# One subtraction between two stages, copies ahead of exponentials in four batches, and the own-token transposes first

## The chip, the cores and the metric

The kernel runs on one core of a Trainium2 chip. The metric is the device time of one execution in microseconds (us). The profile is one execution recorded by the hardware profiler: its span runs from the first to the last instruction.

## The reference

Four layers, each added to its input. `x` has 64 batches of 64 tokens of 512 numbers. The stage that the change touches is the third layer (attention over a cache of key and value blocks, 8 query heads on 4 key/value heads of 64, a window of 256 keys) with its output projection `Wo`, and the fourth (a small matrix per batch).

```
x = x + _L0_cond_ref(x, itok_B_0_15, L0_cond_W, L0_cond_b)
x = x + _L1_cond_ref(x, L1_cond_W, L1_cond_A, L1_cond_Bm, L1_cond_scalings, itok_B_0_6)
x = x + _L2_cond_ref(x, L2_cond_Wq, ..., itok_Bx257_0_4111, itok_B_37_3939)
x = x + _L3_cond_ref(x, itok_B_0_7, L3_cond_weights, fside_8xS_0)
...
scores = jnp.einsum('bghtd,bgsd->bghts', qg, k_all) * SCALE
scores = jnp.where(allowed[:, None, None, :, :], scores, -jnp.inf)
p = jax.nn.softmax(scores, axis=-1)
o = jnp.einsum('bghts,bgsd->bghtd', p, v_all).reshape(Bx, H, Tx, HD)
o = o.transpose(0, 2, 1, 3).reshape(Bx, Tx, H * HD)
return jnp.einsum('bto,do->btd', o, Wo)
```

## The kernel before

The kernel has two stages, each a software pipeline written out by hand. Every engine has its own program, and only semaphores tie them together. An engine works through its program strictly in the order in which it is written, so an instruction that waits holds all that stand behind it.

Stage one (`phase_one`, 32 pairs of batches, until about 514 us) computes layers 0 and 1 and the queries, keys and values of layer 2. It writes new keys and values to `new_rows` in DRAM.

Stage two (`phase_two`) runs once for each of the 64 batches, with a few steps more for what trails behind. Step `b` works on several batches at once. The names below are those of the code.

- **GpSimd (POOL)** gathers the keys and values of later batches into `ring` (called `kv` there): `gather_new` issues three indirect DMAs for each batch (L535, then L546 twice), `gather_old` one (L499). They are paced by semaphores of the batches in work.
- **TensorE (PE)**, step `b`: `scores(b)` (L753, twelve records in the profile, into three PSUM banks); `transpose_keys(b+1, .., 0)` (L730, L731); on even steps from 4 on the second half of `project` (L802); `transpose_probs` of batch `b-1` (L771: eight 128x128 transposes of window probabilities in two groups of four; L777: two of the batch's own 64 tokens); `transpose_keys(b+1, .., 1)`; on odd steps from 3 on the first half of `project`; on even steps the matmul of layer 3 (L838); `values` of batch `b-1` (L790, L795), which waits for all three copies of transposed probabilities.
- **ScalarE (ACT)**: copies the transposed keys from PSUM into `kt` (`copy_keys`, L920, once for each of two halves; `scores(b+1)` waits for both); takes four exponentials (`exps`, L930); copies the second group of transposed probabilities and the own ones (`copy_second` L937, `copy_own` L942, into `pt` and `pt2`); copies the attention output (`ot_hi`, L964). How many of the four exponentials stand ahead of the probability copies is `early`: one on odd steps, all four on even ones. The second copy of keys stands behind all of them.
- **VectorE (DVE)**: adds the mask and takes the row minimum for four heads' groups (`masked`, L1236); copies the first group of transposed probabilities (`copy_first`, L1218), behind all four `masked` on even steps and between them on odd ones; on even steps from 4 on adds into `x3` (L1261); scales the four groups of probabilities (L1272), each adding one to `prob_ready`; makes the next mask (L1205, L1206); computes the remainder of the attention output (`ot_lo`, L1224).

`Wo` is used as two parts: `wo_hi`, which ScalarE makes at L913 between the stages, and the remainder `wo_lo` (L1279), four subtractions of 128x512 each. `wo_lo` is first read by `project` of step 3.

The semaphore `pt_done` counts three for each batch, one at the end of each group of transposes. Whoever copies a group waits for its number, and `gather_new` and the exponentials of a later batch wait for the third.

Of the kernel before, what the change touches and what calls it, by code (L numbers as in the profile page):

```python
# [4 lines left out]
F32 = mybir.dt.float32  # L5
# [50 lines left out]
def build(nc, a):  # L56

    ctx = ExitStack()
    with ctx:
# [187 lines left out]
        def wait(eng, semaphore, value):  # L247

            if not isinstance(value, int) or value > 0:
                eng.wait_ge(semaphore, value)  # L250
# [309 lines left out]
        def _(pe):  # L560
# [177 lines left out]
            def phase_two(b, j, s):  # L738
# [25 lines left out]
                def transpose_probs():  # L764

                    for p, copied in ((0, pt0_ready), (1, pt1_ready)):
                        pe.wait_ge(prob_ready, G * b - G + 2 * p + 2)
                        wait(pe, copied, b - 1)
                        for q in range(2):
                            for c in range(2):  # L770
                                last = nc.tensor.transpose(ps_pt[p][:, (q * 2 + c) * P:(q * 2 + c + 1) * P],  # L771
                                                           prob[:, r % 2, (5 * p + 3 * q + c) * P:(5 * p + 3 * q + c + 1) * P], ident[:, :])
                        last.then_inc(pt_done, 1)
                    wait(pe, pt2_ready, b - 1)
                    wait(pe, ot_ready, b - 1)
                    for p in range(GP):
                        last = nc.tensor.transpose(ps_pt2[:, p * P:(p + 1) * P], prob[:, r % 2, (5 * p + 2) * P:(5 * p + 3) * P], ident[:, :])  # L777
                    last.then_inc(pt_done, 1)

# [67 lines left out]
        def _(act):  # L847
# [77 lines left out]
            def phase_two(b, j, s):  # L925
# [7 lines left out]
                def copy_second():  # L933

                    act.wait_ge(pt_done, 3 * b - 1)
                    wait(act, pv_done, b - 1)
                    nc.scalar.activation(pt[:, 1, :, :, :].rearrange("p q c t -> p (q c t)"), ps_pt[1][:, :], ACT.Copy).then_inc(pt1_ready, 1)  # L937

                def copy_own():

                    act.wait_ge(pt_done, 3 * b)
                    nc.scalar.activation(pt2[:, :, :].rearrange("p q t -> p (q t)"), ps_pt2[:, 0:GP * P], ACT.Copy).then_inc(pt2_ready, 1)  # L942

                if on(b, -1, NB):
                    copy_keys(b + 1, s + 1, 0)
                early = 1 if s % 2 == 1 else G
                if on(b, 0, NB):
                    for g in range(early):
                        exps(g)
                if on(b, 1, NB):  # L950
                    copy_second()
                    copy_own()
                if on(b, 0, NB):
                    for g in range(early, G):
                        exps(g)
                if on(b, -1, NB):
                    copy_keys(b + 1, s + 1, 1)
# [13 lines left out]
        def _(dve):  # L971
# [230 lines left out]
            def make_mask(b, s):  # L1202
# [4 lines left out]
                                ALU.is_lt, ALU.mult).then_inc(mask_ready, 1)  # L1207

            dve.wait_ge(ld_late, 16)
            dve.wait_ge(ld_mask, 4 * 16)  # L1210
            make_mask(0, 0)

            def phase_two(b, j, s):
                def copy_first():

                    dve.wait_ge(pt_done, 3 * b - 2)
                    wait(dve, pv_done, b - 1)
                    V.tensor_copy(pt[:, 0, :, :, :].rearrange("p q c t -> p (q c t)"), ps_pt[0][:, :]).then_inc(pt0_ready, 1)  # L1218
# [55 lines left out]
                if on(b, -1, NB):  # L1274
                    make_mask(b + 1, s + 1)
                if isinstance(b, int) and b < 2:
                    dve.wait_ge(wo_hi_ready, 1)
                    for c in range(2 * b, 2 * b + 2):
                        V.tensor_tensor(wo_lo[:, c, :], wo_stage[:, c, :], wo_hi[:, c, :].bitcast(F32), ALU.subtract).then_inc(wo_lo_ready, 1)  # L1279
                if on(b, 1, NB):  # L1280
# [78 lines left out]
```

## Time and profile before

| what | value |
|---|---|
| median of 3 runs | 975.33 us (974.92 to 979.87) |
| time of the profiled execution | 973.05 us |
| its span | 970.5 us |
| TensorE busy | 935.1 us (96%) |
| VectorE busy | 604.6 us (62%) |
| ScalarE busy | 383.8 us (40%) |
| GpSimd busy | 513.4 us (53%) |

The span is 2.55 us under that execution's own time, and the median of the three runs is 2.28 us above it. TensorE is busy nearly all the time; the stretches in which it is not are where the order of the other engines can matter.

### The profile page before, as it was taken

The numbers are of one execution on the slowest core, as the hardware profiler recorded it, in microseconds if no ns is written. First come the engines' busy times: TensorE is split into PE (matmuls) and PEld (weight loads), VectorE is DVE, ScalarE is ACT, GpSimd is POOL, SyncE is SP. The second block draws the span as 40 slices with busy tenths as digits, with TensorE's granted clock in tenths as the row PEclk, the third lists the DMA queues.
The fourth block names the chain that finished last, engine by engine and source line by source line (L and its number), as shares of the span: only waits on it lengthen the run. The fifth ranks groups of instructions, "written<-read, shape, count | busy, mean of one in ns | idle before, by whom it ended". The sixth has DMA issues, their size and how long they took to land.

```text
span 970.5 us, 22302 instructions
## 1 busy us (share of the span) xinstructions
PE 935.1 (96%) x6253; PEld 690.1 (71%) x6253; DVE 604.6 (62%) x1788; ACT 383.8 (40%) x1061; POOL 513.4 (53%) x469
## 2 busy tenths in 40 slices
PE   6899999999999999999996899999999999999998
PEld 4566766667666676676765677778778788787785
DVE  6434344657566554446643677777777787777875
ACT  2121221212212122121213556566565665666653
POOL 1255464454644558745366566555665555555530
PEclk9999999999999999999998999999999999999999
DMA  9789888686786776867645565665666666666641
GB/s 305 267 278 306 276 304 277 211 271 224 253 280 220 258 247 229 279 229 253 231 141 164 150 195 176 194 207 175 197 184 192 209 204 198 181 195 210 206 136 45
DMA packets 105162, 212.48 MB, mean 219 GB/s; under 512 B 29563, under 2 KB 52056, under 8 KB 96930
## 3 DMA queue, kind: packets, MB, share of 16 engines
q1 hardware_dynamic: 71042, 145.54, 44.4%
q0 software_dynamic: 25088, 57.74, 20.0%
q10 hardware_dynamic: 8992, 8.73, 2.8%
q8 instruction: 17, 0.28, 0.1%
q14 instruction: 23, 0.19, 0.1%
HBM read 204.39 MB, written 33.86 MB: 245 GB/s over the span
## 4 chain that ended last, share of the span: by engine, by line
PE 92%; DMA 2%; issue 2%; DVE 1%; ACT 1%; POOL 1%; SPq 1%; DVEq 0%; POOLq 0%; ACTq 0%
PE banks L587 11%; PE banks L802 9%; PE banks L705 9%; PE banks L753 9%; PE banks L790 7%; PE banks L626 6%; PE banks L634 6%; PE banks L636 6%; PE banks L771 6%; PE banks L730 4%; PE banks L795 4%; PE banks L695 3%; PE banks L838 3%; PE banks L710 3%; PE banks L597 2%
## 5 line engine op out<-in xcount | busy, mean ns | idle before, releaser
L546 POOL DMA_INDIRECT ring<-new_rows,idx x128 | 130.0, 1016 | 84.1 <-DVE big L1272 54.8
L458 POOL TENSOR_TENSOR rms<-ss,neg_half 128x12 f32<-128x12 f32 x31 | 70.8, 2285 | 175.5 <-DVE ss L1181 175.5
L930 ACT ACTIVATE big<-big,neg_max 128x320 f32<-128x320 f32 x256 | 141.3, 554 | 2.7 <-DVE neg_max L1236 2.5
L1236 DVE CUSTOM_DVE_ANT_0 big<-banks,mask 128x320 f32<-128x320 f32 x256 | 114.7, 486 | 36.0 <-PE banks L753 33.2
L587 PE MATMUL banks<-ring 128*64 128x512 f32 x512 | 117.1, 599 | 2.7 <-DMA ring<-in_w 2.7
L871 ACT ACTIVATE x2t_hi<-banks 128x512 fp32r<-128x512 f32 x32 | 19.1, 597 | 235.2 <-PE banks L597 235.2
L920 ACT ACTIVATE kt<-banks 128x384 f32<-128x384 f32 x128 | 62.1, 485 | 100.7 <-PE banks L731 100.7
L753 PE MATMUL banks<-kt,q_in 64*128 64x128 f32 (+2 forms) x768 | 89.0, 365 | 3.1 <-ACT kt L920 3.1
L587 PEld LDWEIGHTS banks<-ring 128*64 128x64 f32 x512 | 34.1, 136 | 81.0 <-issue 79.9
L535 POOL DMA_INDIRECT ring<-new_rows,idx x64 | 61.5, 961 | 55.1 <-PE banks L777 51.2
L1272 DVE TENSOR_SCALAR big<-big,recip 128x320 f32<-128x320 f32 x256 | 86.0, 398 | 2.3
L790 PEld LDWEIGHTS banks<-pt,ring 128*64 128x64 f32 x1024 | 55.9, 137 | 43.9 <-issue 27.8
L753 PEld LDWEIGHTS banks<-kt,q_in 64*128 64x128 f32 x768 | 74.7, 190 | 16.5 <-issue 14.5
L499 POOL DMA_INDIRECT ring<-in_kvrows,idx x64 | 61.2, 956 | 41.8 <-PE banks L753 24.5
L1134 DVE TENSOR_TENSOR x<-banks,x_in 128x512 f32<-128x512 f32 x32 | 22.1, 691 | 95.1 <-PE banks L587 90.9
L790 PE MATMUL banks<-pt,ring 128*64 128x128 f32 x1024 | 70.6, 279 | 7.7 <-ACT pt L942 3.3
L903 ACT ACTIVATE sq<-banks 128x512 f32<-128x512 f32 x31 | 18.6, 600 | 130.8 <-PE banks L636 130.8
L448 POOL TENSOR_TENSOR x_in<-x_in,bias_in 128x512 f32<-128x512 f32 x32 | 41.6, 1301 | 51.5 <-DMA ring<-in_rope 45.2
L771 PE MATMUL banks<-ident,big 128*128 128x128 f32 x512 | 67.5, 275 | 0.2 <-DVE big L1272 0.2
L634 PE MATMUL banks<-wqkv_hi,x2t_lo 128*128 128x512 f32 x248 | 66.4, 390 | 0.0
L636 PE MATMUL banks<-wqkv_lo,x2t_hi 128*128 128x512 f32 x248 | 66.3, 389 | 0.0
L626 PE MATMUL banks<-wqkv_hi,x2t_hi 128*128 128x512 f32 x248 | 65.4, 405 | 0.7 <-ACT x2t_hi L871 0.7
(169 smaller groups left out, 1982.8 us busy)
## 6 DMA issues: line engine op xcount, KB each, us to landing
ring<-in_w SPq DMA_DIRECT2D x62, 1024.0 KB, 6.0
ring<-in_xt SPq DMA_DIRECT2D x32, 256.0 KB, 2.7
x_in<-in_x SPq DMA_DIRECT2D x32, 256.0 KB, 5.6
bias_in<-in_b SPq DMA_DIRECT2D x64, 128.0 KB, 5.4
x_dram<-x SPq DMA_DIRECT2D x32, 256.0 KB, 5.0
q_dram<-q_t ACTq DMA_DIRECT2D x32, 256.0 KB, 2.3
new_rows<-kv_out SPq DMA_DIRECT2D x32, 256.0 KB, 4.8
q_in<-q_dram SPq DMA_DIRECT2D x64, 128.0 KB
```

The source lines that it names most:

```text
L546: pool.indirect_dma_start(out=kv[:, s, c, :], out_offset=None, in_=new_rows, in_offset=bass.IndirectOffsetOnAxis(ap=idx[:, b, 1 + c:2 + c] ...
L587: last = nc.tensor.matmul(ps_l0[T * h:T * h + T, :], xt[:, s, c, T * h:T * h + T], w0[:, 2 * s + h, c * D:(c + 1) * D], start=(c == 0), st ...
L626: nc.tensor.matmul(ps_out[:, :], x2t_hi[:, c, :], wqkv_hi[:, c, n0:n0 + D], start=(c == 0), stop=False)
L634: nc.tensor.matmul(ps_out[:, :], x2t_lo[:, c, :], wqkv_hi[:, c, n0:n0 + D], start=False, stop=False)
L636: last = nc.tensor.matmul(ps_out[:, :], x2t_hi[:, c, :], wqkv_lo[:, c, n0:n0 + D], start=False, stop=(c == DC - 1))
L705: nc.tensor.matmul(ps_l1[:, :], x_part[:, c, :], w_part[:, c, :], start=(c == 0 and x_part is x1t_hi and w_part is w1_hi), stop=False)
L753: return nc.tensor.matmul(banks[:, S0[g] + n0:S0[g] + n1], q_in[r0:r0 + HD, s % 4, g // 2, :], kt[r0:r0 + HD, s % 2, g // 2, k0 + n0:k0 + ...
L771: last = nc.tensor.transpose(ps_pt[p][:, (q * 2 + c) * P:(q * 2 + c + 1) * P], prob[:, r % 2, (5 * p + 3 * q + c) * P:(5 * p + 3 * q + c + ...
L790: nc.tensor.matmul(ps_o[HD * q:HD * q + HD, p * P:(p + 1) * P], kv[:, r, c, v0:v0 + HD], pt[:, p, q, c, :], start=(c == 0 and p == 0), sto ...
L802: last = nc.tensor.matmul(out[:, n0:n1], o_part[:, pair_s, c, :], w_part[:, c, n0:n1], start=(c == 0 and n == 0), stop=(c == DC - 1 and n ...
L930: nc.scalar.activation(prob[:, s % 2, g * NK:(g + 1) * NK], sm[:, s % 2, g, :], ACT.Exp, bias=neg_max[:, s % 2, g:g + 1], scale=-1.0, accu ...
L1236: V.tensor_tensor_reduce(sm[:, s % 2, g, :], ps_s[g], mask[:, s % 2, k0:k0 + NK], 1.0, 3.0e38, ALU.add, ALU.min, accum_out=neg_max[:, s % ...
```

## The change

Four edits in stage two:

1. The four subtractions for `wo_lo` leave the steps `b` = 0 and 1 (two in each, behind the mask) and stand between the stages, behind stage one and ahead of the first mask.
2. In steps 0 to 3 (`ramp`) ScalarE does one exponential, then the probability copies, then the second copy of keys, then the other three exponentials.
3. `transpose_probs` does the two own-token transposes first, then the two groups of four. All ten now stand behind the waits that the own ones had (`ot_ready`, `pt2_ready`) and behind one wait for all four scaled groups; before, each group of four waited for two of them more.
4. In every step ScalarE makes `copy_own` ahead of `copy_second`.

```diff
                 def transpose_probs():
+                    pe.wait_ge(prob_ready, G * b)
+                    wait(pe, pt2_ready, b - 1)
+                    wait(pe, ot_ready, b - 1)
+                    for p in range(GP):
+                        last = nc.tensor.transpose(ps_pt2[:, p * P:(p + 1) * P], prob[:, r % 2, (5 * p + 2) * P:(5 * p + 3) * P], ident[:, :])
+                    last.then_inc(pt_done, 1)
                     for p, copied in ((0, pt0_ready), (1, pt1_ready)):
-                        pe.wait_ge(prob_ready, G * b - G + 2 * p + 2)
                         wait(pe, copied, b - 1)
...
-                    wait(pe, pt2_ready, b - 1)
-                    wait(pe, ot_ready, b - 1)
-                    for p in range(GP):
-                        last = nc.tensor.transpose(ps_pt2[:, p * P:(p + 1) * P], prob[:, r % 2, (5 * p + 2) * P:(5 * p + 3) * P], ident[:, :])
-                    last.then_inc(pt_done, 1)
...
-                early = 1 if s % 2 == 1 else G
+                ramp = isinstance(b, int) and b < 4
+                early = 1 if s % 2 == 1 or ramp else G
                 if on(b, 0, NB):
                     for g in range(early):
                         exps(g)
                 if on(b, 1, NB):
+                    copy_own()
                     copy_second()
-                    copy_own()
+                if ramp:
+                    copy_keys(b + 1, s + 1, 1)
                 if on(b, 0, NB):
                     for g in range(early, G):
                         exps(g)
-                if on(b, -1, NB):
+                if not ramp and on(b, -1, NB):
                     copy_keys(b + 1, s + 1, 1)
...
+            dve.wait_ge(wo_hi_ready, 1)
+            for c in range(DC):
+                V.tensor_tensor(wo_lo[:, c, :], wo_stage[:, c, :], wo_hi[:, c, :].bitcast(F32), ALU.subtract).then_inc(wo_lo_ready, 1)
             dve.wait_ge(ld_late, 16)
             dve.wait_ge(ld_mask, 4 * 16)
             make_mask(0, 0)
...
-                if isinstance(b, int) and b < 2:
-                    dve.wait_ge(wo_hi_ready, 1)
-                    for c in range(2 * b, 2 * b + 2):
-                        V.tensor_tensor(wo_lo[:, c, :], wo_stage[:, c, :], wo_hi[:, c, :].bitcast(F32), ALU.subtract).then_inc(wo_lo_ready, 1)
```

The waits of the three copies on `pt_done` are renumbered to the new order.

ScalarE, steps 0 and 1 (and the beginning of step 2), before and then with the change; `kt` is a copy of keys, `big` an exponential, `pt` a copy of probabilities:

```order
L930 ACTIVATE big,row_sum<-big,neg_max 128x320 x4
L920 ACTIVATE kt<-banks 128x384 x2
L930 ACTIVATE big,row_sum<-big,neg_max 128x320
L937 ACTIVATE pt<-banks 128x512
L942 ACTIVATE pt<-banks 128x256
L930 ACTIVATE big,row_sum<-big,neg_max 128x320 x3
L920 ACTIVATE kt<-banks 128x384
L964 ACTIVATE ot_hi<-banks 128x4x64
```

```order
L930 ACTIVATE big,row_sum<-big,neg_max 128x320
L920 ACTIVATE kt<-banks 128x384
L930 ACTIVATE big,row_sum<-big,neg_max 128x320 x3
L920 ACTIVATE kt<-banks 128x384
L930 ACTIVATE big,row_sum<-big,neg_max 128x320
L942 ACTIVATE pt<-banks 128x256
L937 ACTIVATE pt<-banks 128x512
L920 ACTIVATE kt<-banks 128x384
L930 ACTIVATE big,row_sum<-big,neg_max 128x320 x3
L967 ACTIVATE ot_hi<-banks 128x4x64
```

In each step one copy of keys moved from behind the last exponential to behind the first, and the small copy (`pt`, 256 wide) moved ahead of the large one.

VectorE, from the last instructions of stage one to the first `masked` of stage two, before and then with the change:

```order
L1117 TENSOR_TENSOR q_rot<-ring,rms 128x512
L1119 COPY scol<-scol 128x1
L1205 COPY mask<-beyond 128x1
L1206 TENSOR_SCALAR mask<-iota,first_key 128x255
L1236 ISA big,neg_max<-banks,mask 128x320
```

```order
L1120 TENSOR_TENSOR q_rot<-ring,rms 128x512
L1122 COPY scol<-scol 128x1
L1214 TENSOR_TENSOR wo_lo<-stage,wo_hi 128x512 x4
L1208 COPY mask<-beyond 128x1
L1209 TENSOR_SCALAR mask<-iota,first_key 128x255
```

The four subtractions now stand directly behind the last instruction of stage one.

TensorE in step 1, from the transposes of keys ahead of `transpose_probs` to `values`, before and then with the change:

```order
L730 MATMUL banks<-ident,ring 128x128 x2
L731 MATMUL banks<-ident,ring 128x2x64
L771 MATMUL banks<-ident,big 128x128 x8
L777 MATMUL banks<-ident,big 128x128 x2
L730 MATMUL banks<-ident,ring 128x128 x2
L731 MATMUL banks<-ident,ring 128x2x64
L790 MATMUL banks<-pt,ring 64x128 x8
```

```order
L730 MATMUL banks<-ident,ring 128x128 x2
L731 MATMUL banks<-ident,ring 128x2x64
L770 MATMUL banks<-ident,big 128x128 x2
L776 MATMUL banks<-ident,big 128x128 x8
L730 MATMUL banks<-ident,ring 128x128 x2
L731 MATMUL banks<-ident,ring 128x2x64
L790 MATMUL banks<-pt,ring 64x128 x8
```

The two own transposes (128 wide, x2) moved ahead of the eight of the window, and nothing else moved. GpSimd's and SyncE's programs are the same in both kernels.

## Rows read from the trace of the kernel before

**Rows 1.** The page: the span.

```profile
span 970.5 us, 22302 instructions
```

**Rows 2.** Busy time by stretch: engines in their order, PEclk, DMA share, GB/s.

```profile
520.00:540.00 20.00, 14.42 (x97) 11.84 (x98) 9.96 (x35) 8.66 (x26) 11.00 (x12) 0.74 0.52 152
540.00:560.00 20.00, 16.75 (x140) 13.31 (x140) 14.15 (x52) 11.90 (x38) 11.48 (x12) 0.91 0.52 155
560.00:580.00 20.00, 19.89 (x185) 16.05 (x180) 14.39 (x51) 12.48 (x39) 12.39 (x13) 1.00 0.58 172
```

**Rows 3.** Timeline of TensorE: start, duration, what, idle before and its releaser.

```profile
523.84 2.50 PE L753 MATMUL banks<-kt,q_in 64*128 64x128 f32 x12 [0.67 <-ACT kt L920]
...
530.39 1.86 PE L753 MATMUL banks<-kt,q_in 64*128 64x128 f32 x12 [2.09 <-ACT kt L920]
...
544.35 1.63 PE L790 MATMUL banks<-pt,ring 128*64 128x128 f32 x16 [2.84 <-ACT pt L942]
...
546.96 1.93 PE L753 MATMUL banks<-kt,q_in 64*128 64x128 f32 x12
...
552.12 1.09 PE L790 MATMUL banks<-pt,ring 128*64 128x128 f32 x16
...
553.73 1.35 PE L753 MATMUL banks<-kt,q_in 64*128 64x128 f32 x12
```

**Rows 4.** The page's costliest groups: busy, mean ns of one, idle before.

```profile
L930 ACT ACTIVATE big<-big,neg_max 128x320 f32<-128x320 f32 x256 | 141.3, 554 | 2.7 <-DVE neg_max L1236 2.5
L920 ACT ACTIVATE kt<-banks 128x384 f32<-128x384 f32 x128 | 62.1, 485 | 100.7 <-PE banks L731 100.7
```

**Rows 5.** Timeline of VectorE in steps 0 to 2.

```profile
531.86 1.29 DVE L1279 TENSOR_TENSOR wo_lo<-stage,wo_hi 128x512 fp32r<-128x512 f32 x2
...
537.49 1.27 DVE L1272 TENSOR_SCALAR big<-big,recip 128x320 f32<-128x320 f32 x4
...
539.00 1.29 DVE L1279 TENSOR_TENSOR wo_lo<-stage,wo_hi 128x512 fp32r<-128x512 f32 x2
...
540.54 0.48 DVE L1236 CUSTOM_DVE_ANT_0 big<-banks,mask 128x320 f32<-128x320 f32 x1
```

**Rows 6.** Timelines between the stages: ScalarE, VectorE, GpSimd.

```profile
511.16 1.92 ACT L913 ACTIVATE wo_hi<-stage 128x2048 fp32r<-128x2048 f32 x1 [0.55 <-ACT q_t L857]
...
516.97 0.15 DVE L1205 COPY mask<-beyond 128x1 f32<-128x1 f32 x1 [3.15 <-DMA mask<-in_own]
...
514.29 1.03 POOL L546 DMA_INDIRECT ring<-new_rows,idx  x1 [0.30 <-issue]
```

**Rows 7.** The chain that ended last, in order of time: start, duration, what.

```profile
515.62 5.08 DMA ring<-new_rows,idx
```

**Rows 8.** Timelines of GpSimd and VectorE at three indirect DMAs.

```profile
387.08 1.30 POOL L441 DMA_INDIRECT table_i<-writer,win_both  x1 [0.16 <-issue]
...
531.83 1.00 POOL L546 DMA_INDIRECT ring<-new_rows,idx  x1 [0.92 <-DVE big L1272]
...
539.27 1.90 POOL L546 DMA_INDIRECT ring<-new_rows,idx  x1 [1.80 <-PE banks L753]
...
386.72 0.75 DVE L1162 TENSOR_TENSOR x1t_lo<-x1t,x1t_hi 128x512 fp32r<-128x512 f32 x1 [0.77 <-ACT x1t L879]
```

**Rows 9.** VectorE and TensorE in a step of the steady part.

```profile
561.58 0.42 DVE L1224 TENSOR_TENSOR ot_lo<-banks,ot_hi 128x256 fp32r<-128x256 f32 x1 [1.24 <-ACT ot_hi L964]
...
562.64 1.04 PE L771 MATMUL banks<-ident,big 128*128 128x128 f32 x8
```

**Rows 10.** TensorE and VectorE behind the last scores.

```profile
956.51 1.25 PE L771 MATMUL banks<-ident,big 128*128 128x128 f32 x8 [0.24 <-DVE big L1272]
957.60 0.38 PE L777 MATMUL banks<-ident,big 128*128 128x128 f32 x2
...
960.84 1.09 PE L790 MATMUL banks<-pt,ring 128*64 128x128 f32 x16 [1.45 <-DVE pt L1218]
...
956.96 0.42 DVE L1224 TENSOR_TENSOR ot_lo<-banks,ot_hi 128x256 fp32r<-128x256 f32 x1
```

More of the change, by code:

```diff
@@ L933, in copy_second @@
                 def copy_second():
-                    act.wait_ge(pt_done, 3 * b - 1)
+                    act.wait_ge(pt_done, 3 * b)
                     wait(act, pv_done, b - 1)
@@ L939, in copy_own @@
                 def copy_own():
-                    act.wait_ge(pt_done, 3 * b)
+                    act.wait_ge(pt_done, 3 * b - 2)
                     nc.scalar.activation(pt2[:, :, :].rearrange("p q t -> p (q t)"), ps_pt2[:, 0:GP * P], ACT.Copy).then_inc(pt2_ready, 1)
@@ L1214, in copy_first @@
                 def copy_first():
-                    dve.wait_ge(pt_done, 3 * b - 2)
+                    dve.wait_ge(pt_done, 3 * b - 1)
                     wait(dve, pv_done, b - 1)
```

## The prediction, before the changed kernel was run

> **What bounds the kernel now.** I read the view by stretches first. From 560 us on TensorE is busy 19.89 us of 20 at the full granted clock [rows 2]: there the time is TensorE's work, which the change neither adds to nor takes from. Around the border of the stages it is not: 14.42 us of 520 to 540 and 16.75 us of 540 to 560, at a mean clock of 0.74 and 0.91 of 2.4 GHz [rows 2], so some stretches ran at 1.2 GHz. TensorE's timeline says what it waits for there. Between the batches' first scores (523.84) and those of batch 4 (553.73) it waits 2.09 us for the second copy of keys and 2.84 us for the copies of probabilities [rows 3]. The reader is to see the cost at the slow clock too: sixteen `values` matmuls take 1.63 us at 544.35 against 1.09 at 552.12, and a set of scores 1.93 at 546.96 against 1.35 at 553.73 [rows 3]. From 553.73 on the steps follow each other with no wait worth the name. So what the change can win lies between 523.84 and 553.73, 29.9 us for four batches. What it can lose lies ahead of it, in the wait of each steady step, and at the end.
>
> **The ramp, edits 1, 2 and 3 together.** I follow the order by hand, on the clock of the profile, with TensorE at 2.4 GHz. Durations: an exponential each 0.55, a copy of keys 0.49 [rows 4]; four `masked` some 1.7 (0.48 each, overlapping a little) [rows 5]; scaling and next mask together 1.5 (539.00 minus 537.49) [rows 5]; `ot_lo` 0.42 [rows 9]; ten transposes 1.1 (1.04 for eight with overlap) [rows 9]; scores 1.35, `values` with its own part 1.6 (553.73 minus 552.12) [rows 3]; transposes of a half of keys some 0.35 to 0.45, estimated from their three matmuls.
> Step 0: scores end at 526.3 [rows 3]. One exponential ends at 528.15, the second half of keys is transposed by 528.35 and copied by 528.9. `scores(1)` start at 529.0 instead of 530.39, 1.4 us earlier. The price is that the other three exponentials end at 530.5 instead of 529.8, and batch 0's probabilities are scaled by 532.2.
> Step 1: edit 3 makes even the first transpose wait for all four scaled groups, so TensorE, done with scores and keys at 530.8, idles until 532.25. It ends the ten at 533.35. `masked(1)` starts at 532.5, with no `wo_lo` ahead of it (1.29 us before [rows 5]). Exponential to 533.6, own copy, second copy from 533.7 to 534.3. `values(0)` runs from 534.4 to 536.0, scores 2 to 537.35. ScalarE, behind the copy of keys (534.7), ends the exponentials at 536.3. Scaling and mask last until 538.1, `ot_lo(0)` until 538.5.
> Step 2: four `masked` from 538.5 to 540.1, against a start of 540.54 behind the second pair of subtractions [rows 5]. The transposes wait for `ot_lo` and run from 538.55 to 539.65. Before, all four exponentials stood ahead of the copies and `values(1)` started at 544.35 [rows 3]. Now ScalarE's copies are done at 540.2, and what comes last is VectorE's `copy_first` behind the four `masked`, at 540.8 (0.7 us long, estimated from 0.42 for half the width [rows 9]). `values(1)` starts at 540.9, 3.5 us earlier, `scores(3)` at 542.5 instead of 546.96, 4.5 us earlier.
> Step 3: exponentials end at 542.2, scaling and mask at 544.0, `ot_lo(1)` at 544.4; ten transposes to 545.55, keys, half a projection (1.4), `values(2)` to 548.9. `scores(4)` start there instead of 553.73: **4.8 us earlier**. Behind it TensorE is the bound, as before, and an offset is kept to the end.
> That is with the clock at 2.4 GHz throughout. In this account TensorE still waits 1.45, 0.8, 1.2 and 0.9 us, and before, the clock fell behind gaps of 2.09 and 2.84 us. If `values(2)` and what follows run at 1.2 GHz as they partly did for batch 1 before, the two differences above, 0.54 for sixteen matmuls and 0.58 for a set of scores, with a like amount in its small neighbours, give back 1.1 to 1.8 us. Bounds of the ramp: a gain of 3.0 to 4.8 us. I take 4.3, since the new gaps are all shorter than the two behind which the clock fell.
>
> **Edit 1 at its new place.** `wo_hi` is complete at 513.08, VectorE is free at 513.8 (its idle time of 3.15 us ends at 516.97) [rows 6], so four subtractions (2.5 us, from two of 1.29) end at 516.3 and hold nobody on VectorE. But GpSimd issues the indirect DMAs for batch 0 at that very time: one at 514.29 [rows 6], the last at 515.62. TensorE's first transposes wait for that last one, which lands at 520.70 [rows 7], which is on the chain that ended last. There are two longer indirect DMAs that began while a VectorE subtraction of two SBUF tensors was running. The one at 539.27 took 1.90 us and the subtractions ended at 540.29, 1.02 after it began; the one at 387.08 took 1.30 and the subtraction (386.72 plus 0.75) ended 0.39 after it began [rows 5, 8]. The one at 514.29 took 1.03 with VectorE idle. The excess, 0.87 and 0.27, is nearly what was left of the subtraction. With the subtractions in progress until 516.3, the DMA at 514.29 would finish near 517.3 instead of 515.3, and the one behind it as much later: 2.0 us at most. Below, nothing: where GpSimd's instruction began first, it is not held (531.83, 1.00 us, with a subtraction from 531.86 on [rows 5, 8]). Landing may slip less than the issue, as the 5.08 us contain traffic of other queues. I take **1.6 us later**, near the upper end, because both rows with this order of starts show it.
> The Trainium skill, page "GPSIMD Engine Reference", section "1. Specifications", says the SBUF interfaces are shared with VectorE, with contention for instructions with two SBUF inputs. By that rule the full hold of 2.0 us would be counted, where a reading that VectorE's idle time is free gives 0. The two rows agree with it in kind.
>
> **Edit 3 in the steady part.** The own transposes waited for `ot_lo` behind the eight; now the eight wait as well. In the tight steps (the ones with no projection ahead) `ot_lo` ends at 562.00 and the transposes start at 562.64 [rows 9]: 0.64 us to spare, and scaled probabilities are older still. Cost 0, hidden by scores and keys. If that cover were gone, each 0.1 us would count some thirty times. Edit 4 in the steady part only swaps two neighbours on ScalarE whose last end is what `values` waits for: 0. `gather_new` waits for the third count of `pt_done`, still the end of all ten transposes: 0.
>
> **Edit 3 at the end.** For the last batch no scores hide the wait. The eight started at 956.51 with two of four groups scaled, the own two at 957.60 [rows 10]. Now nothing starts before `ot_lo` is done (956.96 plus 0.42, 957.38), so ten transposes run from 957.42 to 958.5 instead of ending at 957.8. Behind them stand the projection, the sum on VectorE, its copy and `values` at 960.84, one chain to the end [rows 10]. Loss **0.7 us**, between 0.5 and 0.9.
>
> **The sum.** Minus 4.3, plus 1.6, plus 0.7 is minus 2.0 us. Against the profiled execution (973.05, its span of 970.5 [rows 1] and 2.55 around it) that is 971.05; the median of the runs shown lies 2.28 above it, so 973.3.
>
> **Rivals.**
> *The forecast* (0.50): entry held by 1 to 2 us, ramp 3.5 to 4.8: net minus 0.8 to minus 3.1, so 972.2 to 974.5.
> *No hold of the gathers* (0.20): for it speaks the DMA at 531.83, not lengthened; against it the order of starts, since here the subtractions begin at 513.8 and the DMA at 514.29. Net minus 2.8 to minus 4.1: 971.2 to 972.5.
> *The clock falls again, or rises later* (0.13): TensorE's start lies later, so the slow stretch within 520 to 540 [rows 2] can reach further, and the new gaps add up. Ramp 2 to 3, entry 2, tail 0.7: net 0 to plus 0.7, with a second slow stretch up to plus 2: 975.3 to 977.3.
> *The edits are swallowed* (0.07): keys and values are gathered only a little ahead, and GpSimd's last gather for batch 3 waits for scaled probabilities of batch 0, which come 0.65 us later in my account. It was issued at 531.83 in 1.00 us [rows 8], and the one of batch 0 landed 4.1 us after its issue ended (520.70 minus 516.6 [rows 7]). So it lands near 537.6, where TensorE wants it at 537.35. If landings grow longer than that, step 2 and its followers hang on them, the ramp's gain is 1 to 2 us, and entry and tail eat it: 975 to 976.5.
> *The other side, a steady wait* (0.07): transposes of the tight steps wait for `ot_lo` in the new order. It decides once the 0.64 us are used up; at 0.2 us over, thirty such steps cost 6 us, less 2.0: 979.3.
> *A larger gain* (0.03): no hold and a ramp above 4.8, TensorE's weight loads closing up: below 970.5.
>
> **How the numbers follow.** 973.3 is the first case. The range of 8 in 10 joins the first two and most of the third: 970.9 to 976.6. This kernel's measurement tells about 0.5% (4.9 us) from no change. Faster by more needs nearly the whole ramp with no cost at either end: 0.05. Slower by more needs the steady wait or a clock much worse: 0.06. Within 0.5%: 0.89.
>
> **What would show it.** In the changed profile: first transposes of keys near 522.4 and an indirect DMA of some 3 us near 514.3 (wrong if 520.8 and 1.0); `scores(1)` 5.2 us behind `scores(0)` instead of 6.55; `scores(4)` 25 us behind `scores(0)` instead of 29.9; no wait of TensorE for `ot_lo` between 560 and 950; the last `values` 0.7 us later against the last scores. The prediction is wrong if the clock is low in more of these 25 us than before, or if a steady step is longer than before by a trace of a wait, since thirty of them outweigh all the rest.

## The result: 965.4 us, 0.9% faster

| | before | changed |
|---|---|---|
| median | 975.12 us (973.02 to 979.87, 4 runs) | 965.41 us (962.48 to 966.05, 4 runs) |
| ratio | | 0.9911, interval 0.9882 to 0.9941 |
| profiled execution, its span | 973.05, 970.5 us | 962.48, 960.7 us |

The gain is 9.7 us where I had put 2.0. The page of the changed kernel, its span and its engines:

```profile
span 960.7 us, 22134 instructions
...
PE 931.3 (97%) x6253; PEld 687.7 (72%) x6253; DVE 604.0 (63%) x1788; ACT 383.8 (40%) x1061; POOL 512.8 (53%) x469
```

Busy time by stretch of the changed kernel, columns as in [rows 2]:

```profile
500.00:520.00 20.00, 16.34 (x92) 13.47 (x90) 11.45 (x29) 4.85 (x7) 13.81 (x13) 0.91 0.54 179
520.00:540.00 20.00, 13.23 (x124) 10.53 (x126) 10.44 (x41) 11.77 (x36) 13.68 (x14) 1.00 0.61 184
540.00:560.00 20.00, 19.23 (x174) 15.54 (x172) 14.98 (x53) 12.88 (x42) 12.69 (x13) 1.00 0.57 161
560.00:580.00 20.00, 20.00 (x176) 15.83 (x174) 16.75 (x58) 13.00 (x41) 10.90 (x13) 1.00 0.69 207
```

Two things differ from [rows 2]. From 520 us on the clock is full, where it was 0.74 and 0.91: from 520 to 540, 13.23 busy us of TensorE hold 124 matmuls where 14.42 held 97. And 560 to 580 shows 20.00 busy of 20 where [rows 2] has 19.89: the steady part has lost its small gaps. TensorE's timeline, start, duration, what, idle before and its releaser:

```profile
520.80 0.41 PE L730 MATMUL banks<-ident,ring 128*128 128x128 f32 x2 [0.95 <-DMA ring<-new_rows,idx]
...
523.11 1.36 PE L753 MATMUL banks<-kt,q_in 64*128 64x128 f32 x12 [0.67 <-ACT kt L920]
...
526.75 1.35 PE L753 MATMUL banks<-kt,q_in 64*128 64x128 f32 x12 [0.67 <-ACT kt L920]
...
530.00 0.44 PE L770 MATMUL banks<-ident,big 128*128 128x128 f32 x2 [1.02 <-DVE big L1278]
...
532.38 1.10 PE L790 MATMUL banks<-pt,ring 128*64 128x128 f32 x16 [0.74 <-ACT pt L937]
...
536.63 0.41 PE L770 MATMUL banks<-ident,big 128*128 128x128 f32 x2 [0.80 <-DVE ot_lo L1230]
...
538.78 1.09 PE L790 MATMUL banks<-pt,ring 128*64 128x128 f32 x16 [0.54 <-DVE pt L1224]
...
547.54 1.35 PE L753 MATMUL banks<-kt,q_in 64*128 64x128 f32 x12
```

The waits of 2.09 and 2.84 us in [rows 3] are gone, `scores(4)` start 24.4 us behind `scores(0)` instead of 29.9, and the waits that edit 3 adds are there, shorter than in my account: 1.02 and 0.80 us for 1.45 and 1.2. Where the 9.9 us between the ends of the last instructions (968.31 and 958.43) lie:

| stretch | before | changed | difference |
|---|---|---|---|
| start to `scores(0)` | 523.84 | 523.11 | -0.7 |
| `scores(0)` to `scores(4)` | 29.89 | 24.43 | -5.5 |
| `scores(4)` to `scores(60)` | 375.97 | 371.67 | -4.3 |
| `scores(60)` to the last end | 38.61 | 39.22 | +0.6 |

The third row was to be 0. It is 0.15 us in each of 28 pairs of batches, all of it in the even step. There TensorE waits with `values` for ScalarE's two copies: in all 28 even steps of the first profile for which both rows are there, `values` start 0.62 us behind the small copy's start. First before, TensorE and ScalarE (the view ends at 573.5, so three of the sixteen matmuls are not in its second row):

```profile
571.66 1.02 PE L838 MATMUL banks<-bias_in,bd 128*128 128x512 f32 x2
572.79 0.95 PE L790 MATMUL banks<-pt,ring 128*64 128x128 f32 x13
...
571.69 0.57 ACT L937 ACTIVATE pt<-banks 128x512 f32<-128x512 f32 x1
572.17 0.37 ACT L942 ACTIVATE pt<-banks 128x256 f32<-128x256 f32 x1
```

Then the changed kernel:

```profile
552.04 1.02 PE L838 MATMUL banks<-bias_in,bd 128*128 128x512 f32 x2
553.02 1.09 PE L790 MATMUL banks<-pt,ring 128*64 128x128 f32 x16
...
552.07 0.37 ACT L942 ACTIVATE pt<-banks 128x256 f32<-128x256 f32 x1
552.33 0.58 ACT L937 ACTIVATE pt<-banks 128x512 f32<-128x512 f32 x1
```

The pair of copies takes 0.85 us by its rows in the one order (571.69 to 572.54) and 0.84 in the other (552.07 to 552.91): by the last end the swap is worth nothing, as I had counted. But `values` start 0.25 us after the last end before and 0.11 us after it now; from L838 to L790 it is 1.13 and 0.98. With the large copy last, `values` stand directly behind L838 and no gap is left. That some 0.68 and 0.62 us from a copy's start are what TensorE needs at least shows where it clearly waits for the copy: 532.38 above is 0.68 behind the large copy's start (531.70), 544.35 in [rows 3] is 0.61 behind the small one's (543.74).

### The profile page after: what moved, and what is told of

It reads as the page before. It is cut to its first block, busy times and chain, and to the rows that moved or that the text cites. A ratio compares the mean times of both kernels' runs of the same rounds, so it can differ in the third digit from the quotient of the medians.

```text
span 960.7 us, 22134 instructions
## 1 busy us (share of the span) xinstructions
PE 931.3 (97%) x6253; PEld 687.7 (72%) x6253; DVE 604.0 (63%) x1788; ACT 383.8 (40%) x1061; POOL 512.8 (53%) x469
## 4 chain that ended last, share of the span: by engine, by line
PE 91%; SPq 3%; DMA 2%; issue 1%; DVE 1%; ACT 1%; POOL 0%; DVEq 0%; POOLq 0%; ACTq 0%
PE banks L587 11%; PE banks L802 9%; PE banks L705 9%; PE banks L753 8%; PE banks L790 7%; PE banks L626 6%; PE banks L634 6%; PE banks L636 6%; PE banks L776 6%; PE banks L795 4%; PE banks L730 4%; PE banks L838 3%; PE banks L695 3%; PE banks L710 3%; PE banks L597 2%; PE banks L770 1%
## 5 line engine op out<-in xcount | busy, mean ns | idle before, releaser
L546 POOL DMA_INDIRECT ring<-new_rows,idx x128 | 129.4, 1011 | 82.2 <-DVE big L1278 55.5
L753 PE MATMUL banks<-kt,q_in 64*128 64x128 f32 (+2 forms) x768 | 86.8, 358 | 1.3 <-ACT kt L920 1.3
L753 PEld LDWEIGHTS banks<-kt,q_in 64*128 64x128 f32 x768 | 72.8, 187 | 14.3 <-issue 12.4
L790 PEld LDWEIGHTS banks<-pt,ring 128*64 128x64 f32 x1024 | 55.2, 137 | 37.7 <-DVE pt L1224 23.3
L790 PE MATMUL banks<-pt,ring 128*64 128x128 f32 x1024 | 70.0, 278 | 2.7 <-DVE pt L1224 2.0
```

Of the source, the lines that this page charges most:

```text
L546: pool.indirect_dma_start(out=kv[:, s, c, :], out_offset=None, in_=new_rows, in_offset=bass.IndirectOffsetOnAxis(ap=idx[:, b, 1 + c:2 + c] ...
L753: return nc.tensor.matmul(banks[:, S0[g] + n0:S0[g] + n1], q_in[r0:r0 + HD, s % 4, g // 2, :], kt[r0:r0 + HD, s % 2, g // 2, k0 + n0:k0 + ...
L790: nc.tensor.matmul(ps_o[HD * q:HD * q + HD, p * P:(p + 1) * P], kv[:, r, c, v0:v0 + HD], pt[:, p, q, c, :], start=(c == 0 and p == 0), sto ...
```

## The experiments

The tables read three stretches out of each profile: from the first L753 to the reciprocal on VectorE of batch 6 (**ramp**), from there to that of batch 60, by 27 (**pair**: two batches of the steady part), and from there to the last end (**tail**). In the two kernels so far: before 47.98, 13.424, 34.05; changed 42.36, 13.270, 34.66.

### One edit at a time

The kernel before with edit 4 alone:

```diff
-                    copy_second()
                     copy_own()
+                    copy_second()
```

> The kernel before with edit 4 alone: in every step ScalarE makes the 256-wide own copy ahead of the 512-wide second copy. Theory A (what edit 4 saves in the steady part is the time from the last copy's start to TensorE's values matmul: before, the small copy started 0.48 us behind the large one and values started 0.62 us after that, 1.10 in all; with the small one first the large one starts 0.26 later and values 0.69 after that, 0.95): the distance of scores over two batches falls from 13.43 to 13.27 us, and the whole is 4 to 5 us faster, ratio near 0.995. Theory B (it is the order of the transposes on TensorE, edit 3, that closed the wait): 13.43 us stays, ratio 1.000.

With edit 3 alone (its diff as shown above, the copies' waits renumbered):

> The kernel before with edit 3 alone: own transposes first and all ten behind four scaled groups and ot_lo; ScalarE still makes the large copy first. Theory A: 13.43 us for two batches stays, and only the end is later, by 0.6 to 0.7 us; ratio 1.000 to 1.001. Theory B: two batches take 13.27 us, ratio near 0.996.

With edit 2 alone:

```diff
-                early = 1 if s % 2 == 1 else G
+                ramp = isinstance(b, int) and b < 4
+                early = 1 if s % 2 == 1 or ramp else G
...
+                if ramp:
+                    copy_keys(b + 1, s + 1, 1)
...
-                if on(b, -1, NB):
+                if not ramp and on(b, -1, NB):
```

> The kernel before with edit 2 alone: in steps 0 to 3 one exponential, copies of probabilities, copy of keys, three exponentials. Theory A (most of the gain between the scores of batch 0 and batch 4, 5.5 us with the whole change, is edit 2): 4 to 5 us of it here, two batches still 13.43, ratio near 0.995. Rival (without edit 1 the second pair of wo_lo subtractions still stands ahead of batch 2's masks and takes most of it): 2 us or less, ratio above 0.997.

With edit 1 alone (the four subtractions between the stages, none in steps 0 and 1):

> The kernel before with edit 1 alone: the four subtractions between the stages. Theory A: they are off the path in their new place, one indirect DMA is lengthened by 0.3 to 0.5 us and the landing TensorE waits for doesn't slip; on the old place they cost 0.6 us in step 0 and 1.2 in step 1, so scores 0 to scores 4 are 1 to 2 us shorter, ratio 0.998 to 0.999. Rival, my forecast's term: the start of scores 0 is 1.6 us later, ratio 1.000.

On this and the next two occasions the kernel before itself took 1005 to 1008 us and not 975. They ran on the chips numbered 6, 11 and 6; the last two occasions below, where it took 973.6 and 977.5, ran on the chips 0 and 8. For the first pair no chip is on record.

| kernel | median, us | ratio to before | ramp | pair | tail |
|---|---|---|---|---|---|
| before | 1007.7 | | | | |
| edit 4 | 1004.93 | 0.9977 (0.9957 to 0.9997) | 49.67 | 14.517 | 34.31 |
| edit 3 | 1011.23 | 1.0042 (1.0027 to 1.0057) | 50.02 | 14.806 | 35.85 |
| edit 2 | 1005.27 | 0.9975 (0.9958 to 0.9993) | 48.60 | 14.620 | 34.94 |
| edit 1 | 1007.09 | 0.9993 (0.9976 to 1.001) | 48.16 | 14.532 | 34.96 |

A pair of batches takes 1.1 us more than in either of the first two profiles, whatever the edit. So the runs could not say what they were made for; edit 3 alone costs 3.5 us here, the others are within 0.3%. Edit 2 alone was to bring 4 to 5 us in the ramp and edit 1 alone 1 to 2. Against the 49.29 of the kernel before in the same condition (measured below) they bring 0.7 and 1.1, and edits 1, 2 and 4 together (46.65, on chip 11) 2.6. TensorE's clock in the ramp differs between these profiles (the first scores take 1.36 us with edit 2 alone, 2.50 with edit 1 alone and 2.47 in the kernel before), so these shares are not separated.

### What holds every kernel at 1005 us

The changed kernel again, edit 4 again, a variant, and edits 1, 2 and 4. The variant is the kernel before with three exponentials ahead of the copies on even steps, so that both copies are early enough in either order:

```diff
-                early = 1 if s % 2 == 1 else G
+                early = 1 if s % 2 == 1 else G - 1
```

> The changed kernel once more, beside the others, as the measure for them. If two batches take 13.3 to 13.4 us in the steady part as in the first two profiles: ratio 0.989 to 0.994. If TensorE pauses inside the scores as in the four profiles taken since (two batches 14.3 us), the wait that edit 4 closes lies under that pause, so theory A gives only the part before the scores of batch 4, ratio 0.995.

> The kernel before with edit 4 alone, again, since the first look at it was taken where two batches took 14.3 us. Theory A: where the steady part runs without the pause, two batches take 13.27 us instead of 13.43, ratio 0.995. Theory B: 13.43, ratio 1.000.

> The kernel before with three instead of all four exponentials ahead of the probability copies on even steps, and the copies in the old order. It closes the same wait in another way. Theory A (values on even steps wait for ScalarE's last copy, 0.15 us): the copies come 0.55 us earlier, two batches take 13.27 us, ratio 0.994 to 0.995. Theory B (TensorE's own order): 13.43, ratio 1.000 or worse, since the fourth exponential and the scaled probabilities come 0.75 us later.

> The changed kernel without edit 3: the eight window transposes first, as before, the rest as changed. Theory A (edit 3 brings nothing in the steady part and costs 0.6 us at the end): steady part as with the whole change, 0.5 to 1 us faster than it through the end and the ramp, where transposes no longer wait for ot_lo. Theory B: two batches fall back to 13.43 us, 4 us slower than the whole change.

| kernel | median, us | ratio to before (1005.0) | ramp | pair | tail |
|---|---|---|---|---|---|
| changed | 1006.12 | 1.002 (0.9996 to 1.0044) | 48.53 | 14.623 | 35.16 |
| edit 4 | 1004.81 | 0.9991 (0.9973 to 1.001) | 49.24 | 14.505 | 34.82 |
| three early | 1003.58 | 0.999 (0.9969 to 1.0012) | 50.05 | 14.494 | 33.17 |
| edits 1, 2, 4 | 1002.9 | 0.9973 (0.9951 to 0.9994) | 46.65 | 14.527 | 34.78 |

Here the change brings nothing, and what edit 4 won is not there either: something else ends last. For the same reason the variant with three exponentials could not tell its two theories apart. To see what, the kernel before with a profile of this condition, the changed kernel a third time, and the kernel before with one gather less per batch (the keys and values at odd places of the new rows are left out, so that part of the attention is computed on old data):

> The kernel before itself, traced in the condition of the later runs (about 1005 us instead of 975), to have a reference for them. If that condition is one of the machine and not of the edits, it has the same late signals: once in two batches ScalarE's ot_hi starts 1.3 us or more later behind the last values matmul than the 0.7 us (from its start) of the first profile, and two batches take 14.5 us; ratio 1.000.

> The changed kernel a third time. In the condition of the first runs: ratio 0.990. In that of the later ones: 0.998 to 1.003, two batches 14.6 us, about 0.1 us more than the kernels without edit 3, because ot_lo comes late in the tight steps and all ten transposes now wait for it.

```diff
+                    if c == 1:
+                        continue
...
-                    pe.wait_ge(g_new[s], 48 * (j + 1))
+                    pe.wait_ge(g_new[s], 32 * (j + 1))
```

> The kernel before without the last of GpSimd's three gathers from new_rows in each batch (the odd rows of the window): new keys and values at odd places are left out of the result. Theory (TensorE's completion signals are held while such a gather is in progress: ot_hi starts 1.7 to 1.9 us behind the start of the last gather in 20 of 40 batches): with the gather gone the late ot_hi starts mostly go, two batches take 13.4 to 13.8 us instead of 14.5, ratio 0.97 to 0.98. Rival (the late signals have nothing to do with GpSimd): 14.5 us, ratio 0.999.

The fourth has edits 1, 2 and 4 and 46 instead of 26 transposes of L564 between the stages:

> Edits 1, 2 and 4 without edit 3, and 46 instead of 26 transposes of the identity ahead of the first keys of stage two, so that TensorE has no gap of 1 to 2.6 us there and its clock stays at 2.4 GHz. Theory: compared with edits 1, 2 and 4 alone (0.9973 in the later condition) another 0.7 us, from keys and scores 0 at the full clock; ratio 0.995 to 0.997. Rival: the added transposes run past the landing of the keys, or the clock falls behind them all the same; ratio 0.998.

| kernel | median, us | ratio to before (1006.1) | ramp | pair | tail |
|---|---|---|---|---|---|
| before | 1005.58 | 0.9998 (0.9981 to 1.0016) | 49.29 | 14.490 | 34.89 |
| changed | 1005.24 | 1.000 (0.9981 to 1.0019) | 49.22 | 14.597 | 35.58 |
| one gather less | 972.44 | 0.9656 (0.9628 to 0.9685) | 48.33 | 13.450 | 34.01 |
| edits 1, 2, 4, more L564 | 1002.29 | 0.9952 (0.9933 to 0.9971) | 46.87 | 14.570 | 34.20 |

The added L564 were to give 0.7 us by a full clock at the first scores. These took 1.36 us instead of 2.44, but the clock was low later (0.70 from 535 to 540), and the ramp is 46.87 against 46.65: nothing was won there.

The kernel before in the 1005 us condition, GpSimd, TensorE and ScalarE in one step, the rows in the order of the engines:

```profile
706.47 1.01 POOL L546 DMA_INDIRECT ring<-new_rows,idx  x1 [0.30 <-issue]
...
706.03 0.65 PE L795 MATMUL banks<-pt,ring 64*64 64x128 f32 x8
706.61 1.35 PE L753 MATMUL banks<-kt,q_in 64*128 64x128 f32 x10
708.25 0.48 PE L753 MATMUL banks<-kt,q_in 64*128 64x128 f32 x2 [0.29 <-PE banks L753]
...
708.27 0.38 ACT L964 ACTIVATE ot_hi<-banks 128x256 fp32r<-128x256 f32 x1 [3.23 <-PE banks L795]
```

`values` end at 706.68, but ScalarE, idle for 3.23 us, begins `ot_hi` only at 708.27: 2.24 us behind the start of L795, where in the first profile of this kernel it is never more than 0.79 in the steady part. TensorE's own last two scores stand still until the same moment, 1.8 us after GpSimd's last gather began. Between 555 and 945 us `ot_hi` starts 1.2 us or more behind L795 in 27 of the 54 batches for which both rows are complete, in 24 of them 1.5 to 1.8 us behind the start of a last gather, and not once in 58 in the first profile. Without the second L546 it is 2 in 58, the pair is back to 13.450 and 33.7 us are gone. So the gather (or what GpSimd does at its place) takes part in the hold. It is not all of it: on the following two occasions the unchanged kernel, with its gather, took 973.6 and 977.5 us. These occasions differ in the chip (0 and 8 against 6 and 11), and the two on chip 6 agree (1007.7 and 1006.1). No chip was measured in both conditions, so that it is the chip is likely and not shown.

Why edit 4 wins nothing in this condition the same profile shows, in an even step:

```profile
603.93 1.10 PE L838 MATMUL banks<-bias_in,bd 128*128 128x512 f32 x2 [0.23 <-DVE bias_in L1261]
604.96 1.09 PE L790 MATMUL banks<-pt,ring 128*64 128x128 f32 x16
...
604.04 0.37 ACT L942 ACTIVATE pt<-banks 128x256 f32<-128x256 f32 x1
...
603.10 0.69 DVE L1261 TENSOR_TENSOR bias_in<-banks,x_in 128x512 f32<-128x512 f32 x1 [0.65 <-PE banks L802]
```

Here L838 itself stands waiting for VectorE's sum, and `values` follow it at 1.03 us, 0.92 behind the small copy's start where 0.62 would do. From the transposes of keys to L838 it is 0.31 us in the median (0.10 to 0.12 in every even step of the first profile), and from L838 to L790 it is 1.06, against 1.05 with edit 4 and 1.05 with three early exponentials: the gap that edit 4 closes is not there to close.

The late signal is also what edit 3 pays for. The kernel before with edit 3 alone, a tight step, VectorE's row first:

```profile
708.50 0.42 DVE L1224 TENSOR_TENSOR ot_lo<-banks,ot_hi 128x256 fp32r<-128x256 f32 x1 [2.45 <-ACT ot_hi L964]
...
708.49 0.44 PE L730 MATMUL banks<-ident,ring 128*128 128x128 f32 x2
708.76 0.27 PE L731 MATMUL banks<-ident,ring 128*128 128x128 f32 x1
709.07 0.41 PE L770 MATMUL banks<-ident,big 128*128 128x128 f32 x2
709.32 1.04 PE L776 MATMUL banks<-ident,big 128*128 128x128 f32 x8
```

`ot_lo` ends at 708.92 and the transposes start 0.15 us behind it and 0.58 behind the keys' first; in the kernel before under the same condition they start 0.38 us behind the keys (709.05, keys at 708.67), whether `ot_lo` is done or not. So the 0.64 us of cover in [rows 9] are used up. It is so nearly throughout: in 25 of 26 tight steps with edit 3 the transposes stand 0.15 or 0.16 us behind the end of `ot_lo`, and the mean from keys to transposes is 0.54 us, in the changed kernel under the same condition too, against 0.38 without edit 3. At under 0.2 us the wait carries no mark of a releaser. The pair is 14.806, against 14.517 and 14.532 with edit 4 or 1 alone and 14.490 for the kernel before; 0.19 of this is the wait and transposes that take 0.03 us longer, the rest I did not trace.

### The edits without the last gather

All six leave out the gather as above, so that the hold cannot mask the rest; the first is the base.

> The kernel before without GpSimd's last gather of each batch (as one_gather_less: new keys and values at odd places are left out), as the base for the three beside it. 972 us, two batches 13.45 us.

> The whole change without the last gather (the same part left out). If the base stands for the condition of the first runs: 9 to 10 us under ng_base (ratio to the kernel before 0.956), two batches 13.27 us, 5 to 6 us of it before batch 6. Rival (the first result owed something to those runs alone): under 5 us.

> Edit 4 alone (own copy ahead of the large one) without the last gather (the same part left out). Theory A: two batches 13.27 us instead of 13.45, 4.5 to 5 us under ng_base, and values start 0.94 us behind the first copy's start instead of 1.10. Theory B (TensorE's order): as ng_base.

> Edit 3 alone (own transposes first) without the last gather (the same part left out). Theory A: two batches 13.45 us, 0.6 us over ng_base from the end. Theory B: two batches 13.27 us, 4 us under ng_base.

> Edits 1 and 2 without the last gather (new keys and values at odd places are left out). Theory A: two batches 13.45 us as in ng_base; from scores 0 to batch 6 some 5 us less than ng_base (48.3), so the whole 4 to 5 us under ng_base, 966 us where ng_base takes 970.5. Rival (the ramp needs own-first order to pay): under 3 us.

> Edits 1, 2 and 4 without the last gather (the same part left out). Theory A: two batches 13.27 us, the end 0.6 us shorter than ng_whole, transposes of the first batches not held by ot_lo: 960.5 to 961.5 us where ng_whole takes 961.8. Rival (edit 3 also brings something in the ramp, since the own copy can start earlier): 963 us or more.

| kernel | median, us | ratio to before | ramp | pair | tail |
|---|---|---|---|---|---|
| base | 970.47 | 0.998 (0.9961 to 0.9999) | 46.43 | 13.427 | 34.01 |
| all four edits | 961.77 | 0.9893 (0.9852 to 0.9933) | 42.01 | 13.270 | 34.65 |
| edit 4 | 964.73 | 0.9915 (0.9886 to 0.9945) | 46.04 | 13.270 | 33.83 |
| edit 3 | 969.72 | 0.9964 (0.9946 to 0.9981) | 45.13 | 13.435 | 34.84 |
| edits 1, 2 | 970.98 | 0.9932 (0.9906 to 0.9958) | 41.44 | 13.424 | 34.00 |
| edits 1, 2, 4 | 965.61 | 0.9875 (0.9841 to 0.9908) | 41.29 | 13.270 | 33.84 |

The first four ran beside a kernel before of 973.62 us, the last two beside one of 977.53, and their stage one ended 7.5 to 9.2 us later in the profile (first keys at 528.91 and 527.27 against 519.72 of the base); so across the two occasions only stretches and ratios may be compared. With the base, everything is as in the first pair: 13.427 and 13.270, and all four edits are 8.7 us faster.

The pair separates the edits sharply: 13.27 in the three kernels with edit 4, 13.42 to 13.44 in the three without. The base in an even step, TensorE and then ScalarE (this file's lines stand two further down, so L790 is L792):

```profile
568.31 1.02 PE L840 MATMUL banks<-bias_in,bd 128*128 128x512 f32 x2
569.44 1.09 PE L792 MATMUL banks<-pt,ring 128*64 128x128 f32 x16
...
568.33 0.58 ACT L939 ACTIVATE pt<-banks 128x512 f32<-128x512 f32 x1
568.81 0.37 ACT L944 ACTIVATE pt<-banks 128x256 f32<-128x256 f32 x1
```

The same with edit 4 alone:

```profile
567.67 1.02 PE L840 MATMUL banks<-bias_in,bd 128*128 128x512 f32 x2
568.64 1.09 PE L792 MATMUL banks<-pt,ring 128*64 128x128 f32 x16
...
567.69 0.36 ACT L944 ACTIVATE pt<-banks 128x256 f32<-128x256 f32 x1
567.96 0.58 ACT L939 ACTIVATE pt<-banks 128x512 f32<-128x512 f32 x1
```

1.13 us from L840 to L792 become 0.97. Over the steady part the mean distances between the starts of all other groups of TensorE's instructions (keys, transposes, projection, `values`, scores) agree between the two kernels to 0.01 us, so this is the swap and nothing else. It is worth 0.157 us a pair, 4.2 us over the 27 pairs, with 0.4 in the ramp and 0.2 in the tail 4.8 in the profile, and 5.7 between the medians.

## Why the prediction was wrong, by its steps

**The step that failed: edit 4 in the steady part.** It was put as "Edit 4 in the steady part only swaps two neighbours on ScalarE whose last end is what `values` waits for: 0". The two rows' ends do agree to 0.01 us; what TensorE waits for is not the end in the row. It starts 0.25 us after it with the small copy last and 0.11 us or less with the large one last. The size is -4.2 to -4.8 us, nearly half of the result and most of the 5.5 us between the low end of my range (970.9) and 965.4. The trace of before could have said so: every even step of it has 1.13 us from L838 to L790, where two matmuls that last 1.02 us leave no reason for it (rows of TensorE that follow each other unhindered start about when the one ahead ends, or a little sooner), and the 19.89 and not 20.00 in [rows 2] is this gap. I read both as "no wait worth the name" because the trace prints no idle time so short.
The Trainium skill, page "Perfetto Trace Analysis", section "Per-engine timelines", says that the reported end of a ScalarE instruction is when its writes are acknowledged and the semaphore's update is sent, and that its way to the waiting engine is not in the record. The trace agrees that something follows the end: 0.24 us at 544.35 in [rows 3], 0.09 us at 532.38. The page gives no figure for that way and names nothing that it depends on; that it differs with the size or order of the copies only the rows show, and why it does is open.

**The ramp** (4.3 forecast, bounds 3.0 to 4.8): the mechanism was right and the size nearly. Where the first scores run at the full clock in both kernels, `scores(1)` come 1.4 us earlier, as written (5.06 and 3.63 us behind `scores(0)`), and all four edits win 4.4 us in the ramp (46.43 to 42.01), edits 1 and 2 alone 5.0 (41.44). Part of this is again the clock: behind its waits of 2.09 and 2.84 us the base still ran low (granted 0.87 from 530 to 535, 0.83 from 540 to 550), and all four edits ran at 1.00 from 520 to 580. Edit 3 alone wins 1.3 (45.13), where the wait ahead of `values(1)` was 1.98 us and the clock stayed at 1.00 from 540 to 550. Edit 3 costs some 0.7 us on top of the others (41.29 to 42.01), since the transposes wait 1.02 and 0.80 us for scaling and `ot_lo`. The first pair of profiles shows 5.5 to `scores(4)`, 5.6 over the ramp, because the clock differed as well: before, `scores(0)` took 2.50 us at the low clock [rows 3], after it 1.36 at the full one. I had named the clock as a loss if it fell again; it came out as a gain, of some 1.2 us in the ramp and of the 0.7 us ahead of `scores(0)` (from the first transposes of keys to `scores(0)` 3.01 us at the low clock and 2.31 at the full one). The rival that the clock falls again did not come true: the low stretch lay ahead of 520 (0.91 in 500 to 520), where it only lengthened the transposes of L564 that wait for a DMA anyway. The base of the last group had the full clock at `scores(0)` without any edit, so I do not put this part down to the change.

**Edit 1 at its new place** (+1.6 forecast, 0 to 2.0): wrong, it is 0. GpSimd and VectorE of the changed kernel:

```profile
514.31 1.03 POOL L546 DMA_INDIRECT ring<-new_rows,idx  x1 [0.30 <-issue]
515.64 1.47 POOL L546 DMA_INDIRECT ring<-new_rows,idx  x1 [0.31 <-issue]
...
513.75 2.49 DVE L1214 TENSOR_TENSOR wo_lo<-stage,wo_hi 128x512 fp32r<-128x512 f32 x4
```

The subtractions ran from 513.75 to 516.24, over the whole first gather and the first 0.60 us of the second. The first, which was to take three microseconds, took 1.03 as before; the second took 1.47 and so about 0.45 more, and TensorE's first transposes started at 520.80 (520.83 before): the landing did not slip. In all six profiles that have edit 1 and the last gather the second takes 1.46 or 1.47 us, and 0.99 or 1.00 in the seven with that gather and without edit 1. The order of starts, on which I had built the hold from two rows, decides nothing. The rule of the Trainium skill that I had weighed there (page "GPSIMD Engine Reference", section "1. Specifications") names contention and gives no size, and the full hold was my reading of it; the trace agrees with it in the 0.45 us at most. The rival "no hold of the gathers" (0.20) was right in that nothing came later by it.

**Edit 3 in the steady part** (0): right where the kernel takes 975 us: pairs of 13.435 with it and 13.427 without, 0.2 us over 27. The rival of a steady wait (0.07) is real in the 1005 us condition, by the condition that it named: once the 0.64 us are used up by the late `ot_hi`, the transposes wait 0.16 us longer, for `ot_lo`, in nearly every tight step (I had put 0.2), and edit 3 alone makes the kernel 0.4% slower. With the other edits it is the same way round: 1002.9 us without it and 1006.12 with it on one occasion.

**Edit 3 at the end** (+0.7, 0.5 to 0.9): right, +0.83 alone and +0.64 with all four; edit 4 gives 0.2 back there, which I did not trace further. In the changed kernel the transposes wait for `ot_lo`, as written:

```profile
946.85 0.41 PE L770 MATMUL banks<-ident,big 128*128 128x128 f32 x2 [1.26 <-DVE ot_lo L1230]
```

**The chances.** The sum with the terms as measured in the last group is -4.4 (ramp, with edits 3 and 4 in it), 0 (entry), -4.2 (pairs) and +0.6 (tail): -8.0, and the clock's share of 1.2 and 0.7 makes the rest of the 9.9. Against my sum of -2.0 that is 4.2 us from the pairs, 1.6 from the entry, 1.9 from the clock and 0.1 each from ramp and tail. "A larger gain" had 0.03, and as a mere extension of the ramp; no rival held the steady part to be improvable, since I had taken TensorE for the bound there. A gap of 0.15 us in a step that repeats thirty times had the size of everything that I had reckoned with care at its border. As to the best order of all four, edits 1, 2 and 4 without 3 are at least as good: 0.9875 against 0.9893 with overlapping intervals, though on two chips, and 0.9973 against 1.002 in the other condition. In the kernel as it computes the reference this was measured in the 1005 us condition only.

## What to carry to other kernels

Where an engine is "97% busy", compare each repeated step with the same instructions back to back, to 0.1 us: gaps under the resolution of the idle column don't show as waits, and thirty of them are worth more than a visible stall. Of two neighbouring copies for one waiter, don't take their last end for the moment at which it can go: measure start to start in both orders, and try the short one first. And when a wait is moved, ask how much cover it has left where the kernel runs slower: edit 3 is free with 0.64 us to spare and costs 3.5 us when a signal comes 1.5 us late.

## What the runs showed of the hardware

In the steady part of all twenty profiles TensorE's `values` start no sooner than 0.67 to 0.69 us after the start of a last ScalarE copy of 128x512 and 0.61 to 0.63 us after that of one of 128x256, though the second occupies ScalarE only 0.26 us and the first 0.48. As the last of two, the short copy costs 0.48 plus 0.62, the long one 0.26 plus 0.68.

The same kernel took 973 to 978 us on three occasions (two of them on the chips 0 and 8) and 1005 to 1008 on three others (chips 6, 11 and 6). In the latter, TensorE's signals, to ScalarE and to itself, come some 1.5 us late in about every second batch, together and mostly 1.5 to 1.8 us after GpSimd's last gather began, and taking out that one gather on chip 6 restores 33.7 us. Whether it is the gather's descriptors, its transfer or its place that holds the signals, and why not on every occasion, was not tried and stays open.
